# Reordering the attention step: weighing directly in front of the next scores, the second half of the projection between the turns, values through the output bank

## The chip, the cores and the metric

One core of one Trainium2 chip. The metric is the device time of one execution in microseconds (us), from the first to the last instruction; the median of several runs stands for a kernel. Engine names as in the profile: PE is TensorE's matrix multiplication and PEld its loading of weights, DVE is VectorE, ACT is ScalarE, POOL is GpSimd, SP is the engine that issues most DMAs. Each engine works through a queue of its own in the order of the program; semaphores tie the queues together.

## What is computed

A block of three parts on 8 sequences of 512 tokens with 128 features each (4096 tokens, all float32): half a mixture-of-experts feed-forward step, attention, and another half of the same feed-forward step. Each part works on the layer norm of its input.

```python
x = x + 0.5 * ffn(layernorm(x))     # 8 experts, best 2 of each token, hidden size 512
x = x + attention(layernorm(x))
x = x + 0.5 * ffn(layernorm(x))

def attention(x, W_qkv, W_out):     # 16 heads of 64
    q, k, v = split(x @ W_qkv)
    q, k = rotary(q), rotary(k)
    scores = q @ k.T * scale        # per head, causal mask
    weights = softmax(scores)
    return (weights @ v, heads side by side) @ W_out
```

## The kernel before

The change lies in `attention` alone, in the order of four engines' programs. It handles one sequence (a group) after the other, and in each group 8 pairs of heads; one pair of one sequence is a *step* `i`, and there are 64 of them (`STEPS`). The 512 queries of a step are four tiles q = 0 to 3 of 128, and because of the mask tile q needs the first (q + 1) x 128 keys.

The stages of a step, by the names in the code, are these:

- `project(n, half)`: three matmuls (the high and low parts of input and weights) for the first or second half of rotation n, into the bank `pj`. DVE's `rotate(n, half)` reads `pj`, multiplies by cosines and sines and writes `turned`; POOL's `rotate(n)` adds the two halves' products (two instructions, L1909); SP moves the sum into QT or KT. Projections run `EARLY` = 3 rotations ahead.
- `scores(i, q0)`: scores of tiles q0 and q0 + 1 into the two banks `s_bank`, then the masks, added by matmuls (L2008). A score bank is free again when the exponents of the tile two before are done.
- DVE's `maximum(i, q)`, then ACT's `exponent(i, q)` (two instructions, one for each head, each followed by a read of its sum), then `normalise_a(i, q)` on DVE (the reciprocal of the sums, and head 0's share) and `normalise_b(i, q)` on POOL (head 1's share).
- `turn_probs(i, qs)`: transposes of the weights, head 0 first, into the banks `pt_bank`; `copy_a` and `copy_last` on ACT and `copy_b` on DVE bring them to `probT`. The turns of tile 2 reuse columns that the copies of tiles 0 and 1 must have read first.
- `weigh(i)`: 16 matmuls of `probT` with the values V into the bank `o_bank`; ACT's `outputs(i)` copies it to OT.
- `out_project(i)`: eight matmul instructions of OT with the output weights into `pj`; DVE's `residual(i)` adds the result to X.
- `values(w, t)`: three matmuls for a tile of V, into `pj` (two early ones into `o_bank`); ACT's `values` copies it to V.

The softmax of step i and the turning and weighing of step i - 1 run in the same pass of the loop. TensorE's order in a pass, written out by hand, is: `scores(i, 0)`; `turn_probs(i - 1, (0, 1))`; `values`; `turn_probs(i - 1, (2,))`; `out_project(i - 2)`; `scores(i, 2)`; `turn_probs(i - 1, (3,))`; `project(i + 3, 0)`; `weigh(i - 1)`; `project(i + 3, 1)`. The bank `pj` has three users, and `projection_bank` makes each wait until the one before has been read.

Between these lie other pieces. In 7 steps the tokens of the next group are turned (`prep.turn`, with `prep.leading` on ACT and `prep.trailing` on DVE, all through `o_bank`), in 4 steps those of the router of the last part (`lead.turn`, `lead.turned`). Seven steps hold statistics of the next group on DVE (`prep.moments`, L1716), seven others those of `lead.statistics` (L667), and `lead_first`, `lead_counted` and `lead_last` spread the routing of the last part over steps 36 to 63 on DVE.

Of the kernel before, what the change touches and what calls it, by code (L numbers as in the profile page):

```python
# [1757 lines left out]
def attention(nc, X, w_hi, w_lo, wo, rope, wts, ys_dram, ident, identb, causal, stats, mean, rstd, tmpa, tmpb, NB,  # L1758
# [9 lines left out]
    with ExitStack() as ctx:  # L1768
# [105 lines left out]
        with nc.Block() as block:  # L1874
# [75 lines left out]
            def _(pe):  # L1950
# [20 lines left out]
                def values(w, t):  # L1971
                    b, half = w // 2, w % 2
                    if w == 0 and t % 2:
                        wait(pe, v_ready, t - 1)
                        bank = o_bank[:, :]
                    else:
                        projection_bank(v_ready, 4 * w + t + 1)
                        bank = pj[:, :]
                    rows = slice(t * P, (t + 1) * P)
# [65 lines left out]
                for i in range(STEPS + 2):  # L2045
                    this, last = i < STEPS, 0 < i <= STEPS
                    if this:
                        scores(i, 0)
# [11 lines left out]
                    if i > 0 and values_of(i)[0] < HALVES:  # L2060
                        values(*values_of(i))
# [5 lines left out]
                    if last:  # L2067
                        turn_probs(i - 1, (2,))
                    if i in TURN:

                        pe.wait_ge(ot_ready, i - 1)
                        prep.turn(pe, TURN[i], o_bank)
                    if i in LEAD_TURNED:
                        pe.wait_ge(ot_ready, i - 1)
                        lead.turn(pe, LEAD_TURNED[i], prep.xn, o_bank)
                    if i >= 2:
                        out_project(i - 2)
                    if this:
                        scores(i, 2)
# [6 lines left out]
                    if i in LEAD_TURNED:  # L2086
                        pe.wait_ge(lead.xts_ready, LEAD_TURNED[i] + 1)
                    if last:
                        weigh(i - 1)
                    if i + EARLY < ROTATIONS:  # L2090
                        project(i + EARLY, 1)

            @block.vector
            def _(dve):
# [17 lines left out]
                def normalise_a(i, q):  # L2112
# [4 lines left out]
                    dve.reciprocal(rec[:, q, :], sums[:, q, :]).then_inc(rec_ready, 1)  # L2117
                    dve.wait_ge(rec_ready, Q + 1)
# [121 lines left out]
                for i in range(STEPS + 2):  # L2240
                    this, last = i < STEPS, 0 < i <= STEPS
                    if 0 < i and i - 1 + EARLY < ROTATIONS:
                        rotate(i - 1 + EARLY, 1)
                    if this:
                        maximum(i, 0)
                    if last:
                        normalise_a(i - 1, 3)
                    if last:
# [4 lines left out]
                    if this:  # L2253
                        maximum(i, 1)
                    if last:
                        copy_b(i - 1, 2)
                    lead_first(i)
                    if i >= 2:
                        residual(i - 2)
                    if i in MEASURE:  # L2260
# [147 lines left out]
```

## Time and profile before

| what | us |
|---|---|
| runs of the kernel before, median of 3 | 1277.3 |
| lowest and highest of them | 1276.87 and 1278.48 |
| the profiled execution's own span | 1277.2 |
| attention loop in it: first score matmul of step 0 to that of step 63 | 270.35 to 1007.06 |
| one step: first score matmul of step 29 to that of step 30 | 608.15 to 619.74 |

How to read the profile: it is one execution. A timeline row gives the start and the length of a run of equal instructions in us from the span's start, the engine, the line of the code, the operation, its output and inputs by the program's names, the shape, and the number merged in it; brackets give the idle time ahead of the first of them, and what ended it by the profile's reckoning ("issue": nothing that the profile shows). Matmuls overlap, so a row's length is longer than the distance to the next row: distances between starts are what a stage costs. DVE's operations, too, are shown to overlap by some 0.08 us. Where the profile shows the loading of weights late, TensorE waited.

### The profile page before, as it was taken

Reading aid. Unit: us, or ns where it says so; the run is one execution under the profiler, and the core shown is the slowest. Engines: PE = TensorE matmul, PEld = TensorE weight load, DVE = VectorE, ACT = ScalarE, POOL = GpSimd, SP = SyncE. Lnnn points to the kernel's source line nnn. Section 1 sums busy time; section 2 is a strip of 40 time slices with the busy share of each in tenths; the row PEclk is TensorE's granted clock in tenths of the full one; section 3 lists DMA queues with packets and bytes.
Section 4 is the critical chain, followed back from the end, with each engine's and each line's share of the span. In section 5 each row is a group of like instructions: output and inputs, shape, how many; then the busy total and the mean of one; then the engine's idle time right before and its main releaser. Section 6 shows DMA issues by size and latency. Waiting matters only on the chain. (4 is left out here: it accounts for less than half of the span.)

```text
span 1277.2 us, 26829 instructions
## 1 busy us (share of the span) xinstructions
PE 1203.9 (94%) x8070; PEld 891.3 (70%) x8070; DVE 903.4 (71%) x1995; ACT 795.7 (62%) x2264; POOL 814.4 (64%) x888
## 2 busy tenths in 40 slices
PE   7799999979999999999999999999999879999992
PEld 6588888856666666666666666666666568888882
DVE  6775344358888888888788987798998767533543
ACT  4665665646667666767676677766656656555552
POOL 4233356158778788788777776677666536766662
PEclk8899999979999999999999999999999969999996
DMA  9034122122222221222222222212212051114223
GB/s 325 26 96 156 53 57 70 40 66 54 61 46 47 59 59 41 52 59 52 47 52 53 58 54 54 67 34 51 51 36 49 17 180 41 49 48 114 61 63 109
DMA packets 87753, 86.44 MB, mean 68 GB/s; under 512 B 11249, under 2 KB 78705, under 8 KB 87233
## 3 DMA queue, kind: packets, MB, share of 16 engines
q1 hardware_dynamic: 76640, 65.50, 19.9%
q0 software_dynamic: 8864, 18.17, 5.3%
q8 instruction: 73, 1.20, 0.4%
q10 hardware_dynamic: 2112, 1.05, 0.3%
q14 instruction: 64, 0.52, 0.1%
HBM read 33.43 MB, written 17.69 MB: 40 GB/s over the span
## 5 line engine op out<-in xcount | busy, mean ns | idle before, releaser
L1915 POOL TENSOR_SCALAR at_prob<-at_prob,at_rec 128x128 f32<-128x128 f32 (+3 forms) x256 | 312.0, 1223 | 167.6 <-DVE at_rec L2117 165.7
L2297 ACT ACTIVATE at_prob<-at_s,at_nb 128x128 f32<-128x128 f32 (+3 forms) x512 | 264.7, 535 | 16.5 <-DVE at_nb L2109 12.9
L2308 ACT ACTIVATE at_probT<-at_pt 128x128 f32<-128x128 f32 (+3 forms) x256 | 105.2, 437 | 227.5 <-PE at_pt L2022 227.5
L790 POOL DMA_INDIRECT f_xb<-xn_dram,f_source x142 | 141.2, 994 | 161.8 <-PE f_b L1285 101.6
L2109 DVE TENSOR_REDUCE at_nb<-at_s 128x2 f32<-128x256 f32 (+3 forms) x256 | 203.3, 815 | 10.6 <-PE at_s L2008 10.6
L1447 DVE TENSOR_TENSOR f_hid<-f_b,f_silu 128x512 f32<-128x512 f32 x142 | 98.5, 693 | 136.5 <-PE f_b L1298 100.0
L2103 DVE TENSOR_TENSOR at_turned<-at_pj,rope 128x1024 f32<-128x1024 f32 x122 | 148.7, 1219 | 56.5 <-PE at_pj L1969 52.8
L2022 PE MATMUL at_pt<-ident,at_prob 128*128 128x128 f32 x1280 | 183.6, 276 | 4.1 <-DVE wts L381 1.0
L2003 PE MATMUL at_s<-at_KT,at_QT 64*128 64x128 f32 (+3 forms) x1024 | 176.0, 462 | 4.0 <-DMA at_KT<-at_probT 2.8
L1909 POOL TENSOR_TENSOR at_R<-at_turned 128x512 f32<-128x512 f32 x126 | 157.4, 1269 | 24.0 <-DVE at_turned L2103 24.0
L2034 PE MATMUL at_o<-at_probT,at_V 128*64 128x512 f32 (+3 forms) x1024 | 152.0, 437 | 10.9 <-ACT at_probT L2315 3.3
L2022 PEld LDWEIGHTS at_pt<-ident,at_prob 128*128 128x128 f32 x1280 | 141.9, 142 | 25.2 <-issue 13.7
L1316 PE MATMUL f_b<-f_down,f_hidT 128*128 x1136 | 149.9, 275 | 0.4 <-issue 0.4
L2034 PEld LDWEIGHTS at_o<-at_probT,at_V 128*64 128x64 f32 x1024 | 80.6, 136 | 93.9 <-issue 71.3
L1316 PEld LDWEIGHTS f_b<-f_down,f_hidT 128*128 128x128 f32 x1136 | 138.0, 192 | 0.9 <-issue 0.9
L2120 DVE TENSOR_SCALAR at_prob<-at_prob,at_rec 128x128 f32<-128x128 f32 (+3 forms) x256 | 124.2, 485 | 9.2
L1367 ACT ACTIVATE f_hidT<-f_b 128x512 f32<-128x512 f32 x142 | 84.7, 597 | 69.1 <-PE f_b L1305 69.0
L1388 ACT ACTIVATE f_silu<-f_b 128x512 f32<-128x512 f32 x142 | 85.1, 600 | 59.2 <-PE f_b L1298 59.1
L2003 PEld LDWEIGHTS at_s<-at_KT,at_QT 64*128 64x128 f32 x1024 | 78.8, 189 | 52.4 <-issue 24.9
L2297 ACT ACTIVATION_READ_ACCUMULATOR at_prob<-at_s,at_nb 128x1 f32 x512 | 109.6, 214 | 0.0
L1247 POOL DMA_INDIRECT ys_dram<-y,f_target x71 | 70.9, 999 | 45.9 <-issue 33.1
L1429 DVE TENSOR_TENSOR f_xt<-f_b,f_xt 128x128 fp32r<-128x128 f32 x142 | 41.3, 291 | 62.5 <-ACT f_xt L1378 62.4
(326 smaller groups left out, 2224.4 us busy)
## 6 DMA issues: line engine op xcount, KB each, us to landing
at_QT<-at_R SPq DMA_DIRECT2D x128, 128.0 KB, 2.4
at_KT<-at_R SPq DMA_DIRECT2D x124, 128.0 KB, 2.4
ys_dram<-y SPq DMA_DIRECT2D x71, 64.0 KB, 1.8
f_down<-down_t SPq DMA_DIRECT2D x2, 2048.0 KB, 9.2
xn_dram<-f_xn SPq DMA_DIRECT2D x12, 256.0 KB, 6.8
f_xb<-xn_dram,f_source POOLq DMA_INDIRECT x142, 2.6
X<-x SPq DMA_DIRECT2D x4, 512.0 KB, 6.1
gate<-gate_t SPq DMA_DIRECT2D x8, 256.0 KB, 5.1
```

The costliest lines, as they stand in the source:

```text
L790: pool.indirect_dma_start(out=xb[j % AHEAD][:, :], out_offset=None, in_=xn_dram, in_offset=bass.IndirectOffsetOnAxis(ap=routing.source[:, ...
L1316: one = pe.matmul(out_bank(j)[:, 0:P], hidT[k][:, c, :], down[:, bass.ds(e, 1), c, :].rearrange("p a d -> p (a d)"), start=(c == 0), stop= ...
L1909: pool.tensor_tensor(rotated_of(n)[:, :, cols], first[:, :, cols], second[:, :, cols], ALU.add).then_inc(r_ready, 1)
L1915: pool.tensor_scalar(w, w, rec[:, q, 1:2], None, ALU.mult).then_inc(probB_ready, 1)
L2003: pe.matmul(s_bank[q % 2][:, h, 0:n], q_tile[rows, q * P:n], k_tile[rows, 0:n], start=True, stop=False)
L2022: one = pe.transpose(pt_bank[h][:, at:at + P], prob[q][:, h, b * P:(b + 1) * P], ident[:, :])
L2034: one = pe.matmul(o_bank[64 * h:64 * h + 64, b * P:SEQ], V[(i // 4) % 2][:, b, 128 * j + 64 * h:128 * j + 64 * h + 64], probT[h][:, b, b * ...
L2103: dve.tensor_tensor(turned_of(n)[half], src, rope[:, half, :, :], ALU.mult).then_inc(rope_ready, 1)
L2109: dve.tensor_reduce(nb[:, q, :], s_bank[q % 2][:, :, 0:(q + 1) * P], axis=AX, op=ALU.max, negate=True).then_inc(nb_ready, 1)
L2120: dve.tensor_scalar(w, w, rec[:, q, 0:1], None, ALU.mult).then_inc(probA_ready, 1)
L2297: act.activation(prob[q][:, h, :], s_bank[q % 2][:, h, 0:n], ACT.Exp, bias=nb[:, q, h:h + 1], scale=1.0, accum_out=sums[:, q, h:h + 1]).th ...
L2308: act.activation(probT[0][:, 0:q + 1, q * P:(q + 1) * P], pt_bank[0][:, at:at + (q + 1) * P].rearrange("p (b r) -> p b r", r=P), ACT.Copy) ...
```

## The change

Four things are moved, and nothing is computed in another way.

- TensorE: `project(i + 2, 1)`, which stood behind `weigh` one pass earlier, comes between `turn_probs(i - 1, (0, 1))` and `turn_probs(i - 1, (2,))`; `values` goes behind the latter and writes to `o_bank`; `scores(i, 2)` comes ahead of `out_project(i - 2)`; `weigh(i - 1)` is the last piece of a pass, with the next `scores(i + 1, 0)` directly behind. Waits on `v_ready` guard `o_bank`.
- DVE: `normalise_a` is split into `invert` (the reciprocal) and the rest; `maximum(i, 1)` comes ahead of the copies; `rotate(i + 2, 1)` goes behind copies 0 and 1, `normalise_a(i - 1, 3)` behind that; `normalise_a(i, 0)` and `(i, 1)` come ahead of the statistics of `prep.moments`; `residual` stands between `maximum(i, 2)` and `maximum(i, 3)`.
- ACT: `exponent(i, 1)` and `copy_a(i - 1, 2)` come ahead of `values`, and `exponent(i, 2)` ahead of `copy_a(i - 1, 3)` and `copy_last(i - 1)`.
- POOL's and SP's programs stay as they are.

```diff
--- before.py
+++ after.py
@@ -1970,12 +1970,13 @@
 
                 def values(w, t):
                     b, half = w // 2, w % 2
-                    if w == 0 and t % 2:
-                        wait(pe, v_ready, t - 1)
-                        bank = o_bank[:, :]
-                    else:
+                    if w == 0 and t % 2 == 0:
                         projection_bank(v_ready, 4 * w + t + 1)
                         bank = pj[:, :]
+                    else:
+                        wait(pe, v_ready, 4 * w + t - 1)
+                        wait(pe, ot_ready, 4 * (w - 1) + t)
+                        bank = o_bank[:, :]
                     rows = slice(t * P, (t + 1) * P)
                     cols = slice(2048 + half * 512, 2048 + (half + 1) * 512)
                     hi, lo = XT[b % 2][:, 0, rows], XT[b % 2][:, 1, rows]
@@ -2044,6 +2045,7 @@
                         values(0, 2 * n - 1)
                 for i in range(STEPS + 2):
                     this, last = i < STEPS, 0 < i <= STEPS
+                    valued = i > 0 and values_of(i)[0] < HALVES
                     if this:
                         scores(i, 0)
 
@@ -2057,8 +2059,8 @@
                         routing.count_tokens(pe, 0, pt_bank[0][:, 3 * P:4 * P], pt_bank[1][:, 3 * P:4 * P])
                     if last:
                         turn_probs(i - 1, (0, 1))
-                    if i > 0 and values_of(i)[0] < HALVES:
-                        values(*values_of(i))
+                    if 0 < i and i - 1 + EARLY < ROTATIONS:
+                        project(i - 1 + EARLY, 1)
                     if i in LEAD_JUDGED:
                         pe.wait_ge(lead.logits_ready, LEAD_JUDGED[i] + 1)
                     if i == LEAD_COUNTED:
@@ -2066,17 +2068,23 @@
                         pe.wait_ge(routing.gap_ready, 1)
                     if last:
                         turn_probs(i - 1, (2,))
+                    if valued:
+                        values(*values_of(i))
+                    if this:
+                        scores(i, 2)
+                    if i >= 2:
+                        out_project(i - 2)
+                    if valued:
+
+                        last_value = 4 * values_of(i)[0] + values_of(i)[1] + 1
                     if i in TURN:
-
+                        pe.wait_ge(v_ready, last_value)
                         pe.wait_ge(ot_ready, i - 1)
                         prep.turn(pe, TURN[i], o_bank)
                     if i in LEAD_TURNED:
+                        pe.wait_ge(v_ready, last_value)
                         pe.wait_ge(ot_ready, i - 1)
                         lead.turn(pe, LEAD_TURNED[i], prep.xn, o_bank)
-                    if i >= 2:
-                        out_project(i - 2)
-                    if this:
-                        scores(i, 2)
                     if last:
                         turn_probs(i - 1, (3,))
                     if i + EARLY < ROTATIONS:
@@ -2085,10 +2093,10 @@
                         pe.wait_ge(prep.lo_ready, TURN[i])
                     if i in LEAD_TURNED:
                         pe.wait_ge(lead.xts_ready, LEAD_TURNED[i] + 1)
+                    if valued:
+                        pe.wait_ge(v_ready, last_value)
                     if last:
                         weigh(i - 1)
-                    if i + EARLY < ROTATIONS:
-                        project(i + EARLY, 1)
 
             @block.vector
             def _(dve):
@@ -2109,12 +2117,15 @@
                     dve.tensor_reduce(nb[:, q, :], s_bank[q % 2][:, :, 0:(q + 1) * P], axis=AX, op=ALU.max,
                                       negate=True).then_inc(nb_ready, 1)
 
+                def invert(i, q):
+                    Q = 4 * i + q
+                    dve.wait_ge(exp_ready, 2 * Q + 2)
+
+                    wait(dve, probB_ready, Q - 3)
+                    dve.reciprocal(rec[:, q, :], sums[:, q, :]).then_inc(rec_ready, 1)
+
                 def normalise_a(i, q):
                     Q = 4 * i + q
-                    dve.wait_ge(exp_ready, 2 * Q + 2)
-
-                    wait(dve, probB_ready, Q - 3)
-                    dve.reciprocal(rec[:, q, :], sums[:, q, :]).then_inc(rec_ready, 1)
                     dve.wait_ge(rec_ready, Q + 1)
                     w = prob[q][:, 0, :]
                     dve.tensor_scalar(w, w, rec[:, q, 0:1], None, ALU.mult).then_inc(probA_ready, 1)
@@ -2239,37 +2250,40 @@
                     rotate(n, 1)
                 for i in range(STEPS + 2):
                     this, last = i < STEPS, 0 < i <= STEPS
-                    if 0 < i and i - 1 + EARLY < ROTATIONS:
-                        rotate(i - 1 + EARLY, 1)
                     if this:
                         maximum(i, 0)
+                        maximum(i, 1)
                     if last:
-                        normalise_a(i - 1, 3)
-                    if last:
+                        invert(i - 1, 3)
                         copy_b(i - 1, 0)
                         copy_b(i - 1, 1)
                     if i == LEAD_COUNTED:
                         lead_counted(i)
-                    if this:
-                        maximum(i, 1)
+                    if 0 < i and i - 1 + EARLY < ROTATIONS:
+                        rotate(i - 1 + EARLY, 1)
                     if last:
+                        normalise_a(i - 1, 3)
                         copy_b(i - 1, 2)
                     lead_first(i)
+                    if this:
+                        invert(i, 0)
+                        normalise_a(i, 0)
+                        invert(i, 1)
+                        normalise_a(i, 1)
+                    if i in MEASURE:
+                        prep.moments(dve, MEASURE[i])
+                    if this:
+                        maximum(i, 2)
                     if i >= 2:
                         residual(i - 2)
-                    if i in MEASURE:
-                        prep.moments(dve, MEASURE[i])
+                    if this:
+                        maximum(i, 3)
                     if i in TURN:
                         prep.trailing(dve, TURN[i], o_bank)
-                    if this:
-                        normalise_a(i, 0)
-                        normalise_a(i, 1)
-                        maximum(i, 2)
-                    if this:
-                        maximum(i, 3)
                     if i + EARLY < ROTATIONS:
                         rotate(i + EARLY, 0)
                     if this:
+                        invert(i, 2)
                         normalise_a(i, 2)
                     if i < 4:
                         shares(i)
@@ -2283,7 +2297,7 @@
                     if w >= 2 and t == 0:
 
                         act.wait_ge(pv_psum, 4 * (w - 1))
-                    bank = o_bank if w == 0 and t % 2 else pj
+                    bank = pj if w == 0 and t % 2 == 0 else o_bank
                     act.activation(V[w % 2][:, t, :], bank[:, :], ACT.Copy).then_inc(v_ready, 1)
 
                 def exponent(i, q):
@@ -2335,20 +2349,21 @@
                         lead.judged(act, LEAD_JUDGED[i], pt_bank[0][:, 3 * P:4 * P])
                     if this:
                         exponent(i, 0)
+                        exponent(i, 1)
+                    if last:
+                        copy_a(i - 1, 2)
                     if i > 0 and values_of(i)[0] < HALVES:
                         values(*values_of(i))
                     if this:
-                        exponent(i, 1)
+                        exponent(i, 2)
                     if i in TURN:
                         prep.leading(act, TURN[i], o_bank)
                     if i in LEAD_TURNED:
                         lead.turned(act, LEAD_TURNED[i], o_bank)
                     if last:
-                        copy_a(i - 1, 2)
                         copy_a(i - 1, 3)
                         copy_last(i - 1)
                     if this:
-                        exponent(i, 2)
                         exponent(i, 3)
                     if last:
                         outputs(i - 1)
```

## Rows read from the trace of the kernel before

**Rows 1.** The page: span, and busy time and share of each engine.

```profile
span 1277.2 us, 26829 instructions
...
PE 1203.9 (94%) x8070; PEld 891.3 (70%) x8070; DVE 903.4 (71%) x1995; ACT 795.7 (62%) x2264; POOL 814.4 (64%) x888
```

**Rows 2.** Timeline of PE, step 29 (start, length, engine, line, operation).

```profile
608.15 0.93 PE L2003 MATMUL at_s<-at_KT,at_QT 64*128 64x128 f32 x8
...
609.83 0.47 PE L1982 MATMUL at_pj<-w_hi,even_XT 128*128 128x512 f32 x1
...
610.60 1.00 PE L2022 MATMUL at_pt<-ident,at_prob 128*128 128x128 f32 x6
611.66 1.13 PE L1990 MATMUL at_pj<-wo,at_OT 128*128 128x128 f32 x8
612.72 1.77 PE L2003 MATMUL at_s<-at_KT,at_QT 64*128 64x384 f32 x8
614.43 0.40 PE L2008 MATMUL at_s<-causal,identb 128*128 128x128 bf16 x4
...
618.84 0.50 PE L1967 MATMUL at_pj<-even_XT,w_hi 128*128 128x512 f32 x1
...
619.74 0.49 PE L2003 MATMUL at_s<-at_KT,at_QT 64*128 64x128 f32 x4
```

**Rows 3.** Timeline of PEld, step 29: loads that came late.

```profile
611.05 0.31 PEld L2022 LDWEIGHTS at_pt<-ident,at_prob 128*128 128x128 f32 x3 [0.20 <-issue]
611.63 0.97 PEld L1990 LDWEIGHTS at_pj<-wo,at_OT 128*128 128x128 f32 x8 [0.26 <-issue]
...
616.51 0.23 PEld L2034 LDWEIGHTS at_o<-at_probT,at_V 128*64 128x64 f32 x4 [0.54 <-issue]
```

**Rows 4.** Timeline of DVE, step 29.

```profile
608.26 1.23 DVE L2103 TENSOR_TENSOR at_turned<-at_pj,rope 128x1024 f32<-128x1024 f32 x1 [1.22 <-PE at_pj L1969]
609.40 0.41 DVE L2109 TENSOR_REDUCE at_nb<-at_s 128x2 f32<-128x256 f32 x1
609.73 0.15 DVE L2117 RECIPROCAL at_rec<-at_sums 128x2 f32<-128x2 f32 x1
609.92 0.49 DVE L2120 TENSOR_SCALAR at_prob<-at_prob,at_rec 128x512 f32<-128x512 f32 x1
610.33 0.61 DVE L2131 COPY at_probT<-at_pt 128x128 f32<-128x128 f32 x2
610.86 0.68 DVE L2109 TENSOR_REDUCE at_nb<-at_s 128x2 f32<-128x512 f32 x1
611.64 0.56 DVE L2131 COPY at_probT<-at_pt 128x384 f32<-128x384 f32 x1
...
614.76 2.08 DVE L2109 TENSOR_REDUCE at_nb<-at_s 128x2 f32<-128x768 f32 x2
```

**Rows 5.** Timeline of ACT, step 29: copies 3 and the exponents behind them.

```profile
615.31 0.60 ACT L2308 ACTIVATE at_probT<-at_pt 128x512 f32<-128x512 f32 x1 [2.33 <-PE at_pt L2022]
...
616.28 0.58 ACT L2297 ACTIVATE at_prob<-at_s,at_nb 128x384 f32<-128x384 f32 x1
...
617.39 0.70 ACT L2297 ACTIVATE at_prob<-at_s,at_nb 128x512 f32<-128x512 f32 x1
```

**Rows 6.** Timeline of POOL, step 29: normalise_b of tile 3.

```profile
609.98 1.85 POOL L1915 TENSOR_SCALAR at_prob<-at_prob,at_rec 128x512 f32<-128x512 f32 x1 [1.82 <-DVE at_rec L2117]
```

**Rows 7.** Timeline of POOL and DVE, step 37: rotation sums beside routing work.

```profile
704.66 2.48 POOL L1909 TENSOR_TENSOR at_R<-at_turned 128x512 f32<-128x512 f32 x2
...
704.96 0.99 DVE L1635 TENSOR_SCALAR tmpb<-tmpb 128x16 f32<-128x16 f32 x1
...
705.99 1.19 DVE L1636 TENSOR_SCALAR tmpa<-tmpa 128x16 f32<-128x16 f32 x1
707.21 0.18 DVE L1637 TENSOR_TENSOR tmpa<-tmpa,tmpb 128x16 f32<-128x16 f32 x1
```

**Rows 8.** Groups of instructions, attention loop: statistics (busy us, mean ns).

```profile
L1716 DVE BATCH_NORM_STATS2 stats<-X 128x6 f32<-128x128 f32 x28 | 6.0, 278 | 0.0
```

More of the change, by code:

```diff
@@ L2110, in maximum @@
                                       negate=True).then_inc(nb_ready, 1)
-                def normalise_a(i, q):
+                def invert(i, q):
                     Q = 4 * i + q
@@ L2117, in normalise_a @@
                     dve.reciprocal(rec[:, q, :], sums[:, q, :]).then_inc(rec_ready, 1)
+                def normalise_a(i, q):
+                    Q = 4 * i + q
                     dve.wait_ge(rec_ready, Q + 1)
```

## The prediction

> **What bounds the kernel now.** I read three views. First the page: TensorE is busy for 94% of the span [rows 1], so the whole kernel is a TensorE kernel. The chain of waits is no help here: it covers the last instructions alone. So I took one step of the attention loop, i = 29, which runs from one `scores(i, 0)` to the next, 608.15 to 619.74 us: 11.58 us [rows 2]. Below, the times of a step are us after its first score matmul (608.15 = 0). There are 64 steps, and nearly all that carry no routing work repeat this one to 0.02 us, so what a step loses or gains counts about 60 times.
>
> In the timeline of the weight loads (they are issued as soon as the matmuls may go, so a gap ahead of one is a wait) there are three places where TensorE stops for another engine [rows 3]. At 2.90 the second half of `turn_probs(2)` waits for DVE's copies of the first turns (they end at 610.94) [rows 3, 4]: about 0.16 us. At 3.48 `out_project` waits until ACT has emptied `pj`, into which the values went: about 0.22. At 8.36 `weigh` waits for ACT's `copy_last`: about 0.3. Together 0.68 us of 11.58; the rest is TensorE's own work and its changeovers. DVE, ACT and POOL have idle time in each step, but they are in-order queues, and the change rearranges two of them.
>
> **What is removed.** All matmuls stay, in another order. Values leave `pj`, so the wait at 3.48 goes (-0.22). The second half of the projection, which stood between `weigh` and the next scores, takes the place of the values between the turns, at the same length: three 512-column matmuls, 609.83 to 610.60, 0.77 us [rows 2]. If nothing else were late, a step would come to 11.58 - 0.68 = 10.9. I now follow who is late next.
>
> **TensorE up to the masks of the second scores.** Project 1 starts at 1.68 and ends at 2.45 [rows 2]. `turn_probs(2)` then needs DVE's copies 0 and 1. DVE now does both early maxima, then `invert`, then the copies: maximum 0 starts at 1.25 [rows 4], 0.33 later maximum 1, 0.60 later the reciprocal (successive DVE operations start some 0.08 before the end shown of the one before), 0.1 later the copies, which end 0.61 on: 2.89, against 2.79 before. With 0.15 to TensorE the second half starts at 3.04 (before 2.94): the wait between the turns stays, 0.1 longer. The turns end at 3.37, the values at 4.10, and after a changeover of 0.08 the second scores take 1.71 (612.72 to 614.43 [rows 2]): the first mask is issued at M = 5.89. It was 6.27; `out_project` now stands behind it.
>
> **From the masks to weigh.** Here is the term that decides. ACT's new order is: exponents 0 and 1, copy 2, values, *exponent 2*, then copies 3 and last, then exponent 3. Before, both copies stood ahead of exponent 2 [rows 5]. Exponent 2 needs maximum 2, which needs the masks. So TensorE waits in `weigh` for this chain: maximum 2 (0.95, the smaller part of the 2.08 that maxima of 768 and 1024 elements take together [rows 4]), 0.05 to ACT, two exponents of 384 columns 1.11 (616.28 to 617.39 [rows 5]), then from copy 3 to the first load of `weigh` 1.20 (615.31 [rows 5] to 616.51 [rows 3]). Sum 3.31 from the start of maximum 2. Maximum 2 can start 0.33 after the first mask (614.43 to 614.76 [rows 2, 4]), so `weigh` cannot start before M + 3.64. TensorE would be ready at about M + 3.05: out_project 0.95, turns 3 0.88, a short wait for `residual` 0.15 (DVE adds it behind maximum 2; project 0 needs `pj` back), project 0 0.77, masks 0.23, changeover. So the wait at `weigh` grows from 0.3 to 0.6.
>
> **DVE is late on top of that.** Its queue between the copies and maximum 2 now holds: rotate 1 from 2.81 to 4.03 (1.23 [rows 4]; its next starts at 3.95), normalise 3 0.41 to 4.36, copy 2 0.48 to 4.84, then reciprocal 0.19, normalise 0, reciprocal 0.19, normalise 1. POOL's program is unchanged: `normalise_b(3)` starts 0.25 after the reciprocal of q = 3 (609.73 to 609.98) and takes 1.85 [rows 4, 6], now 2.43 to 4.28; then its two rotation sums, 2.48 together [rows 7]: about 4.27 to 5.53 and 5.50 to 6.76. DVE comes to normalise 0 at 5.03, in the first of them, and to normalise 1 at about 5.7, in the second. What that costs is in step 37 [rows 7]: a 128x16 DVE operation begun at 704.96 took 0.99 and ended at 705.95, just behind the first sum's end, and the next one, begun at 705.99, took 1.19 and ended 0.04 behind the second sum. A DVE operation on SBUF begun in a rotation sum waits it out, and one slips in between two sums. So normalise 0 ends at 5.6, normalise 1 at about 6.85, and maximum 2 starts at 6.8, not at M + 0.33 = 6.22. The bounds are 6.22 (not held) and 7.25 (below); I take 6.8, as rows 7 show this very pattern.
>
> By the Trainium skill (SBUF - State Buffer, "Who interferes with whom") DVE in a two-port mode and any GpSimd instruction shut each other out for a whole instruction. The trace agrees for the rotation sums [rows 7] and not for `normalise_b`: in step 29 normalise 3 runs 609.92 to 610.41 while POOL's starts at 609.98 [rows 4, 6], both at their usual length. Were the page right for this pair too, the step would be the second rival's.
>
> **Sum of a step.** 6.8 + 3.31 = 10.11 for `weigh`; `weigh` takes 2.33 (616.51 to 618.84 [rows 2, 3]); changeover to the next scores 0.1: 12.54 us, or +0.96. Over 60 steps +57.6. The moved DMAs cost nothing: POOL's sums come some 0.6 us later in a step, and their Q and K are asked for no earlier than at the next step's start, over 5 us later. ACT's `outputs` follows `weigh` at once and has until the next values, over 3 us later.
>
> **Steps with more in them.** The chain through DVE now sets the time, so what lies in front of maximum 2 counts. Four statistics of 0.278 [rows 8], some 0.83 us per step: 7 steps have them behind normalise 1 (+5.8), 7 in front of normalise 0, where the hold hides part (+0.5 each, +3.5). Routing steps 37 to 58 have operations there which are held as in rows 7: +5 over what they cost now. In 11 steps ACT copies turned tokens between exponent 2 and copy 3, a 128x512 copy like the 0.60 one [rows 5]: +0.55 each, +6. The last three score steps have no rotation, +2. Sum +22. Against the profile's own time, 1277.2 us [rows 1], which is the runs' median (1277.3) to 0.1 us: 1277.2 + 57.6 + 22 = 1356.8, **1357 us**.
>
> **Rivals.** (1) *No hold*: normalise 0 and 1 get through, and exponent 2 alone delays the copies. A step is 6.22 + 3.31 + 2.43 = 11.96, +0.38; 60 of them +23, and +16 for the others, as statistics hide partly under the masks: 1316 us. For it: normalise 0 meets one sum at most in the steps shown. Against: POOL's sums and DVE's place are both fixed by the same reciprocal, with over 1 us to spare. (2) *Normalise 3 held too*, by `normalise_b`: from 3.95 to 4.28, which pushes normalise 0 and 1 against later sums: maximum 2 at 7.25, a step 12.99, 60 x 1.41 + 22: 1384 us. Against it: rows 4 and 6 overlap undisturbed. (3) *Faster*: copy 3 isn't held by exponent 2. `weigh` starts when TensorE comes to it, M + 3.05, and a step is 5.89 + 3.05 + 2.43 = 11.37, -0.21; 60 of them -13, with +3 for the special steps: 1267 us. That needs exponent 2 to be done when the turns for copy 3 are, at about M + 1.8; from the rows it is done at M + 2.4 at best, so maximum 2 would have to start 0.6 us before its masks allow. (4) *Nothing changes*: the moved waits happen to add up to the old ones, 1277 us; that takes half of (3)'s shift.
>
> **How the numbers follow.** Forecast 0.60, (1) 0.17, (2) 0.13, (3) 0.07, (4) 0.03. Slower 0.90, faster 0.07, same 0.03, where 0.2% is about what a measurement of this kernel can tell from no change. The range takes in (1) and (2) with a few us for the special steps, 1308 to 1390; it leaves out (3) and (4), 1 in 10, and the rest is what the special steps may miss by.
>
> **What would show it.** Right: a plain step of 12.3 to 12.8 us; TensorE's longest gap in front of `weigh`, above 0.8 us; ACT idle ahead of exponent 2 until DVE's maximum 2, and copy 3 directly behind exponent 2; normalise 0 and 1 on DVE ending just behind POOL's sums, the latter over 0.9 us long; no gap in front of `out_project`. Wrong: maximum 2 starting 0.33 behind its masks (then rival 1); copy 3 starting within 0.1 us of the end of its turns (rival 3); or TensorE's own matmuls taking another time in the new order, which no row of before shows.

## The result, and the profile after

The changed kernel is slower: 1354.6 us against 1277.1, a ratio of 1.0597 (95% interval 1.057 to 1.0623). The prediction was 1357 us. The profiled execution spans 1352.9 us, 75.7 more than that of before.

The page of the changed kernel, span, busy times and one group of instructions (busy us, mean ns, then the idle time ahead and what ended it):

```profile
span 1352.9 us, 26914 instructions
...
PE 1204.7 (89%) x8070; PEld 890.7 (66%) x8070; DVE 926.3 (68%) x1995; ACT 791.3 (58%) x2264; POOL 806.7 (60%) x888
...
L2311 ACT ACTIVATE at_prob<-at_s,at_nb 128x128 f32<-128x128 f32 (+3 forms) x512 | 265.5, 539 | 201.1 <-DVE at_nb L2117 198.7
```

The same group on the page of the kernel before:

```profile
L2297 ACT ACTIVATE at_prob<-at_s,at_nb 128x128 f32<-128x128 f32 (+3 forms) x512 | 264.7, 535 | 16.5 <-DVE at_nb L2109 12.9
```

TensorE is busy for the same time as before [rows 1] in a longer span: what was added is waiting, but for some 10 us of slower clock that the last part of e4 and the account below tell of. And ACT now sits idle 198.7 us in all until a maximum of DVE's is there, where the page of before has 12.9 for the same wait (`nb` holds the maxima). That is over twice the loss; ACT can afford part of this idle time, and the step shows which part it cannot.

Step 29 of the changed kernel, timeline of several engines (start, length, engine, line). It runs from 638.34 to 650.72, 12.38 us where it was 11.58 [rows 2]; of before, [rows 2 to 7] answer to these lines:

```profile
638.34 0.93 PE L2004 MATMUL at_s<-at_KT,at_QT 64*128 64x128 f32 x8
...
640.71 1.56 POOL L1915 TENSOR_SCALAR at_prob<-at_prob,at_rec 128x512 f32<-128x512 f32 x1 [2.29 <-DVE at_rec L2125]
...
641.25 0.31 PEld L2023 LDWEIGHTS at_pt<-ident,at_prob 128*128 128x128 f32 x3 [0.20 <-issue]
...
642.35 2.66 POOL L1909 TENSOR_TENSOR at_R<-at_turned 128x512 f32<-128x512 f32 x2
...
643.24 0.64 DVE L2131 TENSOR_SCALAR at_prob<-at_prob,at_rec 128x128 f32<-128x128 f32 x1
643.80 0.15 DVE L2125 RECIPROCAL at_rec<-at_sums 128x2 f32<-128x2 f32 x1
...
643.98 1.18 DVE L2131 TENSOR_SCALAR at_prob<-at_prob,at_rec 128x256 f32<-128x256 f32 x1
...
644.14 0.40 PE L2009 MATMUL at_s<-causal,identb 128*128 128x128 bf16 x4
644.32 0.97 PEld L1991 LDWEIGHTS at_pj<-wo,at_OT 128*128 128x128 f32 x8
...
645.09 0.94 DVE L2117 TENSOR_REDUCE at_nb<-at_s 128x2 f32<-128x768 f32 x1
...
646.06 0.58 ACT L2311 ACTIVATE at_prob<-at_s,at_nb 128x384 f32<-128x384 f32 x1 [2.92 <-DVE at_nb L2117]
...
646.68 0.19 PEld L1967 LDWEIGHTS at_pj<-even_XT,w_hi 128*128 128x128 f32 x1 [0.56 <-DVE X L2152]
...
647.19 0.59 ACT L2322 ACTIVATE at_probT<-at_pt 128x512 f32<-128x512 f32 x1
...
647.66 0.60 ACT L2329 ACTIVATE at_probT<-at_pt 128x512 f32<-128x512 f32 x1
...
648.38 0.23 PEld L2035 LDWEIGHTS at_o<-at_probT,at_V 128*64 128x64 f32 x4 [1.18 <-issue]
...
650.72 0.49 PE L2004 MATMUL at_s<-at_KT,at_QT 64*128 64x128 f32 x4
```

Read it from the masks of the second scores (L2009, 644.14, that is 5.80 into the step). Maximum 2 (L2117) could follow 0.33 later, as before. It starts at 645.09, because DVE is still in normalise 1 (L2131, 128x256), which takes 1.18 us: it was begun in the second of POOL's two rotation sums (642.35, 2.66 long together) and ends just behind it, as did the two operations of [rows 7]. Exponent 2 (646.06) follows maximum 2, copy 3 (647.19) follows exponent 2 at once, and `weigh` (648.38) follows copy last (647.66). TensorE has then stood idle: the 1.18 ahead of this load is its longest gap in the step; before it was 0.54 [rows 3]. Not every gap ahead of a load is such a wait: the loads of the masks come 0.76 behind the loads before them in both kernels, while the matmuls of the second scores still run. There is no gap in front of `out_project` (644.32) any more, where [rows 3] had 0.26.

### The profile page after: what moved, and what is told of

It is laid out like the page before. It is cut to its first block and busy times, and to the rows that moved or that the text cites. A ratio compares the mean times of both kernels' runs of the same rounds, so it can differ in the third digit from the quotient of the medians.

```text
span 1352.9 us, 26914 instructions
## 1 busy us (share of the span) xinstructions
PE 1204.7 (89%) x8070; PEld 890.7 (66%) x8070; DVE 926.3 (68%) x1995; ACT 791.3 (58%) x2264; POOL 806.7 (60%) x888
## 5 line engine op out<-in xcount | busy, mean ns | idle before, releaser
L1915 POOL TENSOR_SCALAR at_prob<-at_prob,at_rec 128x128 f32<-128x128 f32 (+3 forms) x256 | 293.1, 1149 | 241.0 <-DVE at_rec L2125 239.5
L2311 ACT ACTIVATE at_prob<-at_s,at_nb 128x128 f32<-128x128 f32 (+3 forms) x512 | 265.5, 539 | 201.1 <-DVE at_nb L2117 198.7
L2117 DVE TENSOR_REDUCE at_nb<-at_s 128x2 f32<-128x256 f32 (+3 forms) x256 | 203.3, 816 | 158.7 <-PE at_s L2009 158.6
L2035 PE MATMUL at_o<-at_probT,at_V 128*64 128x512 f32 (+3 forms) x1024 | 162.0, 460 | 58.9 <-ACT at_probT L2329 58.9
L1909 POOL TENSOR_TENSOR at_R<-at_turned 128x512 f32<-128x512 f32 x126 | 167.7, 1351 | 34.0 <-DVE at_turned L2111 29.9
L2035 PEld LDWEIGHTS at_o<-at_probT,at_V 128*64 128x64 f32 x1024 | 84.8, 143 | 147.4 <-issue 118.2
L2131 DVE TENSOR_SCALAR at_prob<-at_prob,at_rec 128x128 f32<-128x128 f32 (+3 forms) x256 | 163.4, 638 | 6.8
L2337 ACT ACTIVATE at_OT<-at_o 128x512 f32<-128x512 f32 x64 | 38.2, 597 | 89.4 <-PE at_o L2035 89.4
```

The source lines that it names most:

```text
L1909: pool.tensor_tensor(rotated_of(n)[:, :, cols], first[:, :, cols], second[:, :, cols], ALU.add).then_inc(r_ready, 1)
L1915: pool.tensor_scalar(w, w, rec[:, q, 1:2], None, ALU.mult).then_inc(probB_ready, 1)
L2035: one = pe.matmul(o_bank[64 * h:64 * h + 64, b * P:SEQ], V[(i // 4) % 2][:, b, 128 * j + 64 * h:128 * j + 64 * h + 64], probT[h][:, b, b * ...
L2117: dve.tensor_reduce(nb[:, q, :], s_bank[q % 2][:, :, 0:(q + 1) * P], axis=AX, op=ALU.max, negate=True).then_inc(nb_ready, 1)
L2131: dve.tensor_scalar(w, w, rec[:, q, 0:1], None, ALU.mult).then_inc(probA_ready, 1)
L2311: act.activation(prob[q][:, h, :], s_bank[q % 2][:, h, 0:n], ACT.Exp, bias=nb[:, q, h:h + 1], scale=1.0, accum_out=sums[:, q, h:h + 1]).th ...
```

## The experiments

Each is told by its plain step (distance between the first score matmuls of steps 29 and 30) and its median. For comparison:

| kernel | plain step, us | median, us | against before (95% interval) |
|---|---|---|---|
| before | 11.58 | 1277.1 | |
| changed | 12.38 | 1354.6 | 1.0597 (1.057 to 1.0623) |
| e1, copies ahead of exponent 2 | 11.54 | 1291.3 | 1.010 (1.008 to 1.012) |
| e2, maximum 2 ahead of normalise 1 | 11.76 | 1310.6 | 1.025 (1.022 to 1.027) |
| e3, POOL's sums later | 11.77 | 1305.1 | 1.022 (1.019 to 1.024) |
| e4, statistics later | 12.38 | 1344.0 | 1.052 (1.049 to 1.055) |
| e6, before with ACT's new order alone | 13.15 | 1394.5 | 1.092 (1.089 to 1.095) |
| e5, e1's and e2's mends together, residual moved as well | 11.14 | 1279.4 | 1.0015 (1.0006 to 1.0025) |
| e7, e5 with the rest moved too | 11.14 | 1263.8 | 0.989 (0.987 to 0.991) |

**e1: is it the copies?** In the changed kernel, ACT takes the copies ahead of exponent 2 again.

```diff
-                    if this:
-                        exponent(i, 2)
...
                     if last:
                         copy_a(i - 1, 3)
                         copy_last(i - 1)
                     if this:
+                        exponent(i, 2)
                         exponent(i, 3)
```

> The changed kernel, with one thing put back: on ACT copy 3 and copy last stand ahead of exponent 2 again. Theory (the chain masks, maximum 2, exponent 2, copies, weigh sets the step): weigh no longer waits for exponent 2. A plain step, 12.38 us in the changed kernel, falls to about 11.5, because weigh then starts when TensorE has done project 0, which still waits for a residual that DVE reaches late; about 1290 us in all. Rival (the copies are not the cause, DVE's held normalise alone is): maximum 2 still starts at 6.75 in a step, the step stays above 12.2, and the time stays above 1340 us.

Measured: 11.54 and 1291.3. Timeline of step 29 (it starts at 611.70):

```profile
617.35 1.18 DVE L2131 TENSOR_SCALAR at_prob<-at_prob,at_rec 128x256 f32<-128x256 f32 x1
...
618.45 0.94 DVE L2117 TENSOR_REDUCE at_nb<-at_s 128x2 f32<-128x768 f32 x1
...
619.31 0.60 ACT L2322 ACTIVATE at_probT<-at_pt 128x512 f32<-128x512 f32 x1 [2.82 <-PE at_pt L2023]
...
620.04 0.19 PEld L1967 LDWEIGHTS at_pj<-even_XT,w_hi 128*128 128x128 f32 x1 [0.57 <-DVE X L2152]
...
620.28 0.58 ACT L2311 ACTIVATE at_prob<-at_s,at_nb 128x384 f32<-128x384 f32 x1
...
620.94 0.20 PEld L2035 LDWEIGHTS at_o<-at_probT,at_V 128*64 128x64 f32 x4 [0.36 <-issue]
```

DVE is as late as in the changed kernel: normalise 1 takes 1.18 again and maximum 2 starts 6.75 into the step. But copy 3 no longer cares, and `weigh` starts 9.24 into the step, not at 10.04. So the chain through exponent 2 carries the loss of the plain step. What is left of DVE's lateness shows ahead of project 0 (620.04), which waits 0.57 for the residual that DVE adds behind maximum 2. The whole stays 1.0% above before although a plain step is 0.04 shorter: steps with statistics or turned tokens still cost some 0.8 more than a plain one.

**e2: is it the held normalise?** In the changed kernel, DVE takes maximum 2 first.

```diff
                         normalise_a(i, 0)
-                        invert(i, 1)
-                        normalise_a(i, 1)
...
                     if this:
                         maximum(i, 2)
+                        invert(i, 1)
+                        normalise_a(i, 1)
```

> The changed kernel, with DVE's maximum 2 put ahead of the reciprocal and normalise of tile 1, the operation that POOL's second rotation sum held for 1.18 us. Theory: maximum 2 starts 0.33 us behind its first mask, at about 6.2 in a step and not at 6.75; everything behind it on the chain comes 0.6 earlier; a plain step is about 11.8 and the whole about 1310 us. Exponent 2 still stands ahead of the copies, so it stays slower than the kernel before. Rival (the hold costs nothing, since exponent 2 or the copies are late for another reason): within 0.5% of the changed kernel's 1354.6 us.

Measured: 11.76 and 1310.6. Timeline of step 29 (from 617.99):

```profile
623.78 0.40 PE L2009 MATMUL at_s<-causal,identb 128*128 128x128 bf16 x4
...
624.10 0.96 DVE L2117 TENSOR_REDUCE at_nb<-at_s 128x2 f32<-128x768 f32 x1 [0.58 <-PE at_s L2009]
...
625.17 0.35 DVE L2131 TENSOR_SCALAR at_prob<-at_prob,at_rec 128x256 f32<-128x256 f32 x1
...
627.42 0.23 PEld L2035 LDWEIGHTS at_o<-at_probT,at_V 128*64 128x64 f32 x4 [0.72 <-issue]
```

Maximum 2 starts 0.32 behind the first mask, 6.11 into the step, and normalise 1, now behind POOL's sums, takes its 0.35. `weigh` starts 9.43 into the step, 0.61 earlier than in the changed kernel, and the step is 0.62 shorter.

**e3: is it POOL's sums that hold it?** e2 also took normalise 1 out of the chain. Here DVE and ACT stay as changed, and POOL does its rotation sums later.

```diff
-                    if 0 < i and i - 1 + EARLY < ROTATIONS:
-                        rotate(i - 1 + EARLY)
                     if i < STEPS:
                         normalise_b(i, 0)
                         normalise_b(i, 1)
+                    if 0 < i and i - 1 + EARLY < ROTATIONS:
+                        rotate(i - 1 + EARLY)
```

> The changed kernel, with POOL's rotation sums moved behind its normalise of tiles 0 and 1, so that no sum runs while DVE normalises these tiles; DVE's and ACT's programs stay as changed. Theory: normalise 1 on DVE takes 0.35 us instead of 1.18, maximum 2 starts at about 6.2, a plain step is about 11.8, the whole about 1310 us, the same as with maximum 2 put first. Rival A (DVE is late from its own queue, not from the sums): maximum 2 stays near 6.75 and the time within 0.5% of 1354.6. Rival B (the sums now deliver Q and K too late): the gap moves to the scores, which wait for a DMA, and the time is not below 1340.

Measured: 11.77 and 1305.1. Timeline of step 29 (from 617.67; this kernel's lines lie one further down):

```profile
622.57 0.29 DVE L2132 TENSOR_SCALAR at_prob<-at_prob,at_rec 128x128 f32<-128x128 f32 x1
622.62 1.73 POOL L1915 TENSOR_SCALAR at_prob<-at_prob,at_rec 128x128 f32<-128x128 f32 x2 [1.02 <-DVE at_rec L2126]
...
622.96 0.35 DVE L2132 TENSOR_SCALAR at_prob<-at_prob,at_rec 128x256 f32<-128x256 f32 x1
...
623.47 0.40 PE L2010 MATMUL at_s<-causal,identb 128*128 128x128 bf16 x4
...
623.79 0.96 DVE L2118 TENSOR_REDUCE at_nb<-at_s 128x2 f32<-128x768 f32 x1 [0.48 <-PE at_s L2010]
624.33 2.51 POOL L1909 TENSOR_TENSOR at_R<-at_turned 128x512 f32<-128x512 f32 x2
```

With no sum beside them, normalise 0 and 1 on DVE take 0.29 and 0.35, in the same place in the same queue in which they took 0.64 and 1.18. Maximum 2 is back at 0.32 behind the masks. The hold by the sums is shown, and its price: 0.61 us a step. The sums' lateness (Q and K) costs nothing in a plain step, which is as long as e2's; steps with turned tokens, such as 28, take 13.43 instead of 12.87, and why stays open.

**e4: what the special steps cost.** Four of the steps with statistics of the next group took 14.84 us, not the 13.4 that the prediction's sum gives them (12.54 and 0.83). Views of step 10 of the changed kernel: its stretch up to `weigh` and `weigh` itself (start, end and length, busy us and instructions of PE, PEld, DVE, ACT and POOL, then the granted clock of TensorE as a share of full speed, then the share and GB/s of the DMAs), and TensorE's timeline:

```profile
393.14:403.95 10.81, 8.98 (x63) 6.12 (x61) 9.55 (x20) 6.05 (x20) 7.55 (x14) 1.00 0.22 49
404.00:407.90 3.90, 3.90 (x16) 1.96 (x16) 0.97 (x3) 1.18 (x4) 1.40 (x1) 0.56 0.02 4
```

```profile
402.25 0.50 PE L1967 MATMUL at_pj<-at_XT,w_hi 128*128 128x512 f32 x1 [1.10 <-DVE X L2152]
...
403.99 4.07 PE L2035 MATMUL at_o<-at_probT,at_V 128*64 128x512 f32 x16 [0.77 <-ACT at_probT L2329]
407.98 0.71 PE L2004 MATMUL at_s<-at_KT,at_QT 64*128 64x128 f32 x6
```

The statistics (0.86) put off maximum 2 and with it the residual: TensorE's matmuls idle 1.10 us ahead of project 0 (0.32 in step 29) and, after three matmuls, 0.77 ahead of `weigh` (as in step 29). Then the granted clock is 0.56, which is about the lower of its two levels, 1.2 of 2.4 GHz, and `weigh` takes 3.99 from start to next scores, not 2.31. In e4 the statistics stand behind the residual.

```diff
-                    if i in MEASURE:
-                        prep.moments(dve, MEASURE[i])
                     if this:
                         maximum(i, 2)
                     if i >= 2:
                         residual(i - 2)
+                    if i in MEASURE:
+                        prep.moments(dve, MEASURE[i])
```

> The changed kernel, with the four statistics of the next group put behind the residual instead of ahead of maximum 2 (7 steps of 64). In the changed kernel four of these steps take 14.84 us, 2.46 more than a plain one, though the statistics take 0.86: in these weigh runs at a granted clock of 0.58 and takes 4.0 us instead of 2.33. Theory: the lateness of 0.86 is what lets the clock fall, so all 2.46 go: these steps come to 12.4, the clock stays at 1.00 in them, and the whole falls by about 13 us to 1342. Rival (the fall of the clock has nothing to do with the statistics): the steps lose 0.86 at most and the whole 6 us at most, to 1349.

Measured: 1344.0, and all seven steps with these statistics lost what they cost; steps 10, 18, 26 and 34 take 12.38 each. The four lost 2.46 each as expected, 9.8 together; the whole is down 10.6. It is not down by the full 13: the other three steps with these statistics gave back 2.2 together, and step 37, whose `weigh` had been slow without these statistics, 1.7; but the slow clock came up elsewhere, and two routing steps, 49 and 56, went from 13.48 and 13.81 to 15.06 and 15.38. TensorE's timeline of step 49 shows the same pattern, an idle of 1.37, three matmuls, an idle of 0.77, and a `weigh` of 3.96 us:

```profile
897.68 0.50 PE L1967 MATMUL at_pj<-even_XT,w_hi 128*128 128x512 f32 x1 [1.37 <-DVE X L2152]
...
899.42 3.96 PE L2035 MATMUL at_o<-at_probT,at_V 128*64 128x512 f32 x16 [0.77 <-ACT at_probT L2329]
```

The same step of the changed kernel:

```profile
909.71 0.50 PE L1967 MATMUL at_pj<-even_XT,w_hi 128*128 128x512 f32 x1 [1.36 <-DVE X L2152]
...
911.45 2.37 PE L2035 MATMUL at_o<-at_probT,at_V 128*64 128x512 f32 x16 [0.77 <-ACT at_probT L2329]
```

So a late residual came ahead of the loss of clock in these steps, but it does not bring it by itself: in the changed kernel step 49 was as late and kept its clock, and so did step 56 (idle of 1.69 and 0.77). Nor does the loss need a late residual: in step 61 of the changed kernel it followed a single idle of 2.75 ahead of `weigh`. Which late step it hits stays open.

**e6: one part of the change alone.** The kernel before, with exponent 2 ahead of copies 3 and last on ACT, and nothing else.

```diff
                     if last:
                         copy_a(i - 1, 2)
+                    if this:
+                        exponent(i, 2)
+                    if last:
                         copy_a(i - 1, 3)
                         copy_last(i - 1)
                     if this:
-                        exponent(i, 2)
                         exponent(i, 3)
```

> The kernel before, with one part of the change alone: ACT takes exponent 2 ahead of copy 3 and copy last. Theory: weigh comes 3.62 us behind the first mask of the second scores (0.33 to maximum 2, 0.95, 1.1 for exponent 2, 1.2 for the copies) and not 2.09: a plain step of 11.58 becomes 13.1, and the whole about 1375 us, slower than the whole change, whose other parts then give some 0.7 us a step back. If the clock falls in each weigh, as it does in the slowest steps of the changed kernel, a step comes to 14.8 and the whole to about 1470. Rival (the place of exponent 2 costs nothing): 1277 us, within 0.5%.

Measured: 13.15 and 1394.5. Timeline of step 29 (from 651.09):

```profile
657.37 0.40 PE L2008 MATMUL at_s<-causal,identb 128*128 128x128 bf16 x4
...
659.82 0.60 ACT L2308 ACTIVATE at_probT<-at_pt 128x512 f32<-128x512 f32 x1
...
661.02 0.23 PEld L2034 LDWEIGHTS at_o<-at_probT,at_V 128*64 128x64 f32 x4 [2.11 <-issue]
...
661.05 2.37 PE L2034 MATMUL at_o<-at_probT,at_V 128*64 128x512 f32 x16 [1.71 <-ACT at_probT L2315]
```

`weigh` starts 3.65 us behind the first mask, where [rows 2, 3] had 2.08. This one move costs a plain step 1.57; the whole change costs 0.80, so its other parts, the hold among them, give 0.77 back by difference, about the 0.7 expected. The total was missed by 20 us: the clock held in plain steps, with an idle of 1.71 ahead of `weigh`, but fell in steps such as 42, 49, 50 and 56, with an idle of 2.15 to 3.08 there; these take 15.3 to 16.2.

**e5: the order on TensorE with both causes mended.** e1's edit, and on DVE normalise 0, maximum 2, residual, then normalise 1 and the statistics.

```diff
                         normalise_a(i, 0)
+                        maximum(i, 2)
+                    if i >= 2:
+                        residual(i - 2)
+                    if this:
                         invert(i, 1)
                         normalise_a(i, 1)
                     if i in MEASURE:
                         prep.moments(dve, MEASURE[i])
-                    if this:
-                        maximum(i, 2)
-                    if i >= 2:
-                        residual(i - 2)
```

> The changed kernel's order on TensorE, with two things mended: on ACT the copies stand ahead of exponent 2, and on DVE the order is normalise 0, maximum 2, residual, then normalise 1 and the statistics. Theory: both causes of the loss are gone and the gain of the order on TensorE is left: weigh starts at about 8.7 in a step, a plain step is 11.1 to 11.3, the whole 1250 to 1262 us, faster than the kernel before. Rival (the new order on TensorE itself costs time, for instance by its changeovers or by copies between the turns that come 0.1 later): a plain step of 11.58 or more and 1277 us or more.

Measured: 1279.4, no better than before, though a plain step is 11.14 as expected. The gain of 0.44 a step is there in the plain steps; seven others, in which the next group's tokens are turned, take 13.77. Step 28 is one of them, from 594.51. Timelines of TensorE (its waits) and of ACT:

```profile
598.48 0.84 PE L2023 MATMUL at_pt<-ident,at_prob 128*128 128x128 f32 x6 [1.35 <-ACT at_probT L2322]
...
605.97 2.37 PE L2035 MATMUL at_o<-at_probT,at_V 128*64 128x512 f32 x16 [0.96 <-DVE even_XT L1754]
```

```profile
596.26 1.65 ACT L1738 ACTIVATE at_xn<-X,at_shift,rstd 128x128 f32<-128x128 f32 x4 [1.04 <-POOL at_shift L1730]
```

ACT normalises the next tokens behind `outputs`, but POOL's factors for it come only 1.75 us into the step (596.26), so copies 0 and 1 of the turns queue behind it and TensorE waits 1.35. Later `weigh` waits 0.96 for DVE's `trailing`, which stands behind maximum 3. In the kernel before, project 1 stood between `weigh` and the next scores, so that ACT's normalising began 0.27 ahead of this step and the copies were not held, and `trailing` stood ahead of both maxima.

**e7: these pieces moved as well.** On ACT the next tokens are normalised in the step of their turn, behind the values, and no longer at the end of the step before:

```diff
                         values(*values_of(i))
                     if i in TURN:
...
+                        prep.normalise(act, TURN[i])
                         prep.leading(act, TURN[i], o_bank)
...
-                        prep.normalise(act, NORMALISE[i])
```

On DVE the routing work of `lead_first` goes behind normalise 1, and `trailing` ahead of maximum 3:

```diff
-                    lead_first(i)
...
                         normalise_a(i, 1)
+                    lead_first(i)
                     if i in MEASURE:
                         prep.moments(dve, MEASURE[i])
-                    if this:
-                        maximum(i, 3)
                     if i in TURN:
                         prep.trailing(dve, TURN[i], o_bank)
+                    if this:
+                        maximum(i, 3)
```

> The combined kernel (order on TensorE as changed, copies ahead of exponent 2, maximum 2 and residual ahead of normalise 1), with the pieces between the steps moved out of its way. In the combined kernel a plain step takes 11.14 us, 0.44 less than before, but 7 steps take 13.77: in them ACT's normalising of the next tokens waits for POOL until 1.8 us into the step and so holds up copies 0 and 1 (TensorE waits 1.35), and weigh waits 0.96 for DVE's trailing part, which stands behind maximum 3. Here ACT normalises in the idle stretch behind the values, trailing stands ahead of maximum 3, and statistics and routing work stand behind normalise 1. Theory (these waits, and nothing else, ate the gain of the plain steps): the 7 steps fall to about 11.3 to 11.7, those with statistics from 11.87 to 11.2, and the whole to 1254 to 1262 us, below the kernel before. Rival (the order on TensorE loses elsewhere, or the moved pieces are late in the new places): 1270 us or more.

Measured: 1263.8 us, 1.1% faster than before, 2 us outside what was expected. A plain step of it, 29, from 600.26 to 611.41:

```profile
606.05 0.40 PE L2009 MATMUL at_s<-causal,identb 128*128 128x128 bf16 x4
...
606.38 0.96 DVE L2117 TENSOR_REDUCE at_nb<-at_s 128x2 f32<-128x768 f32 x1 [0.58 <-PE at_s L2009]
...
608.23 0.35 DVE L2131 TENSOR_SCALAR at_prob<-at_prob,at_rec 128x256 f32<-128x256 f32 x1
...
609.07 0.23 PEld L2035 LDWEIGHTS at_o<-at_probT,at_V 128*64 128x64 f32 x4 [0.36 <-issue]
```

Maximum 2 follows the masks by 0.33, normalise 1 is free of the sums, and the wait ahead of `weigh` is 0.36, changeover included. The steps with turned tokens take 12.04, not 11.3 to 11.7, and those with `lead.statistics` 11.54 rather than 11.2: that is what is missing; what holds them stays open.

## Why the prediction was right

**The term that decides** held: the chain from maximum 2 to `weigh` was forecast at 3.31 us and measured 3.29 (645.09 to 648.38); maximum 2 was forecast 6.8 into the step and started at 6.75. e1 shows that the chain is the cause, e2 and e3 that the hold is its second half.

**The plain step** was forecast at 12.54 and came to 12.38. Of the 0.16, 0.10 is a changeover between `weigh` and the next scores that isn't there: from the first load of `weigh` to the next scores it is 2.33, with no more behind it. 0.05 is maximum 2 and 0.02 the chain.

**Terms that were off without effect.** The copies between the turns were forecast 0.1 later; the load behind them starts 2.91 into the step (641.25), where it was 2.90: the early maxima started 1.18 into the step, not 1.25, and the copies followed the reciprocal 0.03 sooner than was put down. The first mask came at 5.80, not 5.89. Project 0's wait for the residual was put at 0.15 and is 0.56 (646.68), but `weigh` is later anyway; in e1, where it isn't, this wait is what is left.

**Special steps** were mis-sized: in the profiled execution 60 plain steps of +0.80 are 48 us, so 28 came from elsewhere, where 22 were forecast. `lead.statistics` fits (+0.40, forecast 0.5). Turned tokens cost less than was put down: their 7 steps lost 1.14 each, 0.34 more than a plain step, where 0.55 was forecast. The steps with `prep.moments` cost more: 0.83 was forecast, the four plainest lost 2.46, and about 1.7 of that is the clock, which no term held. The clock fell in steps 37 and 61 too, so that six slow `weigh`s make some 10 of the 28 us. The surplus of the plain steps, 9.6, happened to be about as large as that. That the total came within 2.4 us is luck; the mechanism and the plain step are not.

**The reading of normalise_b was wrong.** The prediction took it as undisturbed beside normalise 3 [rows 4, 6]. Groups of instructions by shape for POOL between 280 and 1000 us, first the changed kernel, then the kernel before:

```profile
L1909 POOL TENSOR_TENSOR at_R<-at_turned 128x512 f32<-128x512 f32 x112 | 149.2, 1352 | 9.6 <-DVE at_turned L2111 6.0
L1915 POOL TENSOR_SCALAR at_prob<-at_prob,at_rec 128x512 f32<-128x512 f32 x56 | 87.7, 1566 | 145.9 <-DVE at_rec L2125 145.9
```

```profile
L1909 POOL TENSOR_TENSOR at_R<-at_turned 128x512 f32<-128x512 f32 x122 | 152.4, 1268 | 0.0
L1915 POOL TENSOR_SCALAR at_prob<-at_prob,at_rec 128x512 f32<-128x512 f32 x62 | 115.1, 1857 | 103.1 <-DVE at_rec L2117 103.1
```

`normalise_b` of tile 3 takes 1.57 us in the changed kernel, where normalise 3 comes later, and took 1.86 when it started 0.06 behind it, with 0.43 of normalise 3 still to run: 0.29 of [rows 6]'s 1.85 were a wait, shown as length and not as idle time. By the Trainium skill (SBUF - State Buffer, "Who interferes with whom") the later of such a pair waits for the earlier; for POOL behind DVE the trace now agrees in part, with 0.29 of the 0.43. It doesn't for DVE behind `normalise_b`: in e3, DVE's normalise 1, begun at 622.96 inside POOL's two (622.62 to 624.35), takes 0.35. The second rival, which rested on that direction, isn't borne out, and maximum 2 came at 6.75, not at its 7.25. `normalise_b` ended earlier than forecast for this reason, so the sums came 0.26 earlier, at 4.01 into the step; they were 0.18 longer as a pair, and normalise 1 ended where it was expected. One rule of the prediction is too wide: not every DVE operation on SBUF begun in a sum waits it out. The reciprocal of tile 1 (643.80) takes its usual 0.15 inside the second sum. The sum of the step had put it down at that price, so nothing hung on it.

**Rivals.** "No hold" gave 11.96 for its step; e2 and e3, which take the hold away, show 11.76. "Faster" gave 11.37 for a step in which copy 3 isn't held; e1 shows 11.54, with the residual's wait in it. Both mechanisms are real, and neither was this kernel's state.

## What to carry to other kernels

A wait that is removed from the bottleneck engine pays only if the in-order queues of its helpers deliver in the new order: follow each helper's queue instruction by instruction, and ask of every operation that moved ahead of an urgent one what *it* waits for. A single exponent ahead of two copies cost 1.57 us a step alone (e6). And a new order needs all the rare steps' work moved along with it: e5 had the faster plain step and gained nothing until e7 moved the rest.

## What the runs showed of the hardware

DVE's scaling of a 128x256 tile takes 0.35 us beside POOL's scalings (e3) and 1.18 when it is begun in a POOL addition of two tiles (changed kernel); a reciprocal of 128x2, begun in the same addition, takes 0.15 and is not held. POOL's scaling of 128x512 takes 1.57 when no DVE scaling runs at its start and 1.86 begun just behind one. Between two back-to-back POOL additions one held DVE scaling got through (643.24, 0.64).

TensorE's granted clock fell to 0.56 in a `weigh` that came after an idle of 1.10 us, three matmuls and an idle of 0.77, which made it 1.7 us longer. It fell as well after a single idle of 2.75 (changed kernel, step 61) and of 2.15 to 3.08 (e6). It did not fall after a single idle of 1.71 (e6), nor after idles of 1.35 and 0.96 that lay over 6 us apart (e5), nor in steps 49 and 56 of the changed kernel, after an idle of 1.36 and 1.69, three matmuls and an idle of 0.77. What tells these cases apart stays open here.
